# Quarters of expert products in halves, spread over the border between two blocks

## What is computed

```python
x = x + gnn(layernorm(x), edge_attr, edge_index, ...)      # stages ahead of the mixture
y = layernorm(x)                                           # then, by groups g of t = 16 rows:
logits = einsum('bgtd,des->bgtes', grouped, controller) + tie
perm   = (logits == max(logits, axis=t))                   # one row of the group per expert and set
inner  = relu(einsum of f1 (d,e,s,f=32) with the chosen rows)
inter2 = einsum('bgesf,esfd->bgesd', inner, f2)
result = einsum('bgesd,bgtes->bgtd', inter2, perm)         # back to the rows
out    = x + result
```

## Time and profile before

| | |
|---|---|
| median of 3 runs | 1958.4 us |
| the profiled execution | 1965.0 us, its span 1963.3 us |
| mean granted TensorE clock in it | 0.97 |
| TensorE busy in the span | 1824.5 us, 93% |
| VectorE, ScalarE, GpSimd busy | 1170.8, 988.4 and 356.6 us |
| mixture | from about 1150 us to the end |

### The profile page before, as it was taken

How to read it: one execution, slowest core, us unless ns; L and a number is a source line. 1 busy time by engine, 2 the same in 40 slices (tenths; PEclk the granted TensorE clock), 3 DMA queues, 4 the chain that set the end, 5 groups by cost and what they waited for, 6 DMA issues and landing times. The chain is left out here.

```text
span 1963.3 us, 40727 instructions
## 1 busy us (share of the span) xinstructions
PE 1824.5 (93%) x15580; PEld 1320.5 (67%) x15580; DVE 1170.8 (60%) x2339; ACT 988.4 (50%) x1716; POOL 356.6 (18%) x387
## 2 busy tenths in 40 slices
PE   5487699999999989999999977999999999999999
PEld 3344578888888878888888866555555565665554
DVE  6488466666666544333333336767767777777665
ACT  2355123333333366556655524766657667666653
POOL 4476220000000000000000024222223223222210
PEclk9787899999999999999999989999999999999999
DMA  9987755566666374334433357555546555556433
GB/s 368 301 163 107 169 168 167 167 177 183 180 179 179 122 275 149 126 127 162 150 125 125 116 163 242 161 156 176 163 150 196 154 164 180 164 171 181 136 111 114
DMA packets 246960, 332.09 MB, mean 169 GB/s; under 512 B 58049, under 2 KB 170177, under 8 KB 243618
## 3 DMA queue, kind: packets, MB, share of 16 engines
q1 hardware_dynamic: 237855, 309.11, 50.4%
q0 software_dynamic: 8960, 20.98, 5.6%
HBM read 189.43 MB, written 140.61 MB: 168 GB/s over the span
## 5 line engine op out<-in xcount | busy, mean ns | idle before, releaser
L1535 PE MATMUL bank<-f2s,inner_bd 128*32 128x512 f32 x2528 | 295.8, 598 | 0.6 <-issue 0.4
L599 ACT ACTIVATE h1o<-bank,b_by_channel 128x500 f32<-128x500 f32 x160 | 108.5, 678 | 324.6 <-PE bank L431 316.1
L1434 ACT ACTIVATE inter_hi<-bank 128x512 fp32r<-128x512 f32 x316 | 189.2, 599 | 162.6 <-PE bank L1535 161.6
L1356 DVE TENSOR_TENSOR inter_lo<-bank,inter_hi 128x512 fp32r<-128x512 f32 x316 | 216.2, 689 | 68.0 <-ACT inter_hi L1434 63.2
L429 PE MATMUL bank<-hhi,w_hi 128*128 128x500 f32 x624 | 244.5, 392 | 0.0
L431 PE MATMUL bank<-hhi,w_lo 128*128 128x500 f32 x624 | 243.5, 390 | 0.0
L430 PE MATMUL bank<-hlo,w_hi 128*128 128x500 f32 x624 | 242.6, 389 | 0.0
L429 PE MATMUL bank<-ahi,w_hi 128*128 128x500 f32 x608 | 237.3, 390 | 0.0
L430 PE MATMUL bank<-alo,w_hi 128*128 128x500 f32 x608 | 236.6, 389 | 0.0
L431 PE MATMUL bank<-ahi,w_lo 128*128 128x500 f32 x608 | 236.4, 389 | 0.0
L563 DVE BATCH_NORM_STATS2 stats<-h1o 128x500 f32 (+1 forms) x160 | 103.2, 674 | 155.5 <-ACT h1o L599 155.5
(11 more groups left out here) (140 smaller groups left out, 3240.7 us busy)
## 6 DMA issues: line engine op xcount, KB each, us to landing
h1T<-h1o SPq DMA_DIRECT2D x19, 2000.0 KB, 8.1
h1in<-h1T SPq DMA_DIRECT2D x19, 2000.0 KB, 9.7
aggregate<-at SPq DMA_DIRECT2D x20, 1024.0 KB, 8.9
x<-in_x SPq DMA_DIRECT2D x79, 256.0 KB, 3.2
x<-x SPq DMA_DIRECT2D x79, 256.0 KB, 3.6
back_f<-selection SPq DMA_DIRECT2D x79, 256.0 KB, 3.2
x_back<-x SPq DMA_DIRECT2D x79, 256.0 KB, 3.3
out<-x_back SPq DMA_DIRECT2D x79, 256.0 KB, 2.2
```

What stands on the lines that cost most here:

```text
L599: nc.scalar.activation(h1o[b][:, m, :], mb[m % 4][:, 0:CW], ACT.Identity, bias=b1c[:, m:m + 1]).then_inc(evr, 1)
L1356: nc.vector.tensor_tensor(ilo[b][:, :], bI[b][:, :], ihi[b][:, :].bitcast(F32), ALU.subtract).then_inc(ilr, 1)
L1434: nc.scalar.activation(ihi[b][:, :], bI[b][:, :], ACT.Copy).then_inc(ihr, 1)
L1535: last = nc.tensor.matmul(bI[b][32 * i:32 * i + 32, :], ibd[:, e, j, :, :].rearrange("p s g -> p (s g)"), f2s[:, e, :], start=True, stop=True)
```

## The change

Each quarter is done in two halves of two experts (a step "inner_head", then "inner" for the second half), only the second of which tells VectorE and ScalarE that the quarter is done. Waits stand ahead of the first half. At the borders the halves have other steps between them. For TensorE the order at a regular border becomes: sums; unit 1; unit 2; half 1a; unit 3; 1b; unit 4; 2a; turn_x; 2b; turn_g; logits; 3a; final; 3b; then spread; unit 1; 4a; unit 2; 4b; turn_g; unit 3; unit 4; and on as before. At the first border: 2a; turn_g; 2b; unit 1; 3a; unit 2; 3b; 4a; 4b; unit 3. The ReLU of quarter 2 moves ahead of the new tile's addition and statistics on VectorE, and on SyncE and VectorE turn_g and stats move behind that quarter. Quarter 4 goes to bank `bD[1]`; it waits for quarter 2's ReLU, which is long done, and for the addition of the old block's last tile. Work and its amount are the same.

```diff
--- before.py
+++ after.py
@@ -904,7 +904,7 @@
 
             return bY[::-1] if crossing(kb, j) else bY
 
-        bQ = [bD[0], bD[1], bD[0], bD[0]]
+        bQ = [bD[0], bD[1], bD[0], bD[1]]
         bL, bP = bB[:, 0:P], bB[:, 0:P]
 
         wctl, wf2 = sem("controller_loaded"), sem("f2_loaded")
@@ -1023,25 +1023,31 @@
                 if crossing(back, m):
                     if ahead:
                         yield "sums", m
-                    for p in range(3):
-                        yield "unit", u + p
-                        yield "low", u + p
-                        if p == 1 and next_:
-                            yield "norm", m + 2
+                    yield "unit", u
+                    yield "low", u
+                    yield "unit", u + 1
+                    yield "low", u + 1
+                    if next_:
+                        yield "norm", m + 2
+                    yield "inner_head", (front, 0)
+                    yield "unit", u + 2
+                    yield "low", u + 2
                     yield "inner", (front, 0)
                     yield "unit", u + 3
                     yield "low", u + 3
+                    yield "inner_head", (front, 1)
                     if next_:
                         yield "turn_x", m + 2
+                    yield "inner", (front, 1)
                     if new:
                         yield "turn_g", m + 3
                         yield "stats", m + 3
-                    yield "inner", (front, 1)
                 elif behind and m == 0 and back > 0:
                     yield "unit", u
                     yield "low", u
                     if next_:
                         yield "norm", m + 2
+                    yield "inner_head", (back, 3)
                     yield "unit", u + 1
                     yield "low", u + 1
                     yield "inner", (back, 3)
@@ -1058,18 +1064,21 @@
                     if next_:
                         yield "turn_x", m + 2
                 elif behind and m == 0:
+                    yield "inner_head", (back, 1)
+                    if new:
+                        yield "turn_g", m + 3
                     yield "inner", (back, 1)
                     yield "unit", u
                     yield "low", u
                     if next_:
                         yield "norm", m + 2
-                    if new:
-                        yield "turn_g", m + 3
-                    yield "inner", (back, 2)
+                    yield "inner_head", (back, 2)
                     yield "unit", u + 1
                     yield "low", u + 1
+                    yield "inner", (back, 2)
                     if new:
                         yield "stats", m + 3
+                    yield "inner_head", (back, 3)
                     yield "inner", (back, 3)
                     yield "unit", u + 2
                     yield "low", u + 2
@@ -1125,12 +1134,15 @@
                     yield "select", (m + 1) // 2
                 if exists(front, m + 4 + m % 2):
                     yield "silu", ((m + 4 + m % 2) // 2, (1 - m % 2) * KH // 2, (2 - m % 2) * KH // 2)
+                if crossing(back, m):
+                    yield "inner_head", (front, 2)
                 if behind:
                     yield "final", m
                     yield "result", m
                 if crossing(back, m):
                     yield "inner", (front, 2)
             if front is not None and back is None:
+                yield "inner_head", (front, 0)
                 yield "inner", (front, 0)
 
         def relu(op, q, s, *more):
@@ -1552,19 +1564,20 @@
                         nc.tensor.matmul(bF[:, :], rbd[j % 2][:, b, :], ilo[b][:, :], start=False, stop=(b == QB - 1))\
                             .then_inc(fp, 1)
 
-                def inner(k, q):
-
-                    if q == 0:
+                def inner(k, q, half):
+
+                    if q == 0 and half == 0:
                         if static(k, 1):
                             pe.wait_ge(wf1, 16 * KH)
                         pe.wait_ge(yr, (k * TB + tiles(k)) * KH)
-                    if q == 1 and not static(k, 1):
+                    if q == 1 and half == 0 and not static(k, 1):
                         pe.wait_ge(otr, k * TB - 1)
-                    if q >= 2:
-                        last = 0 if q == 2 else 2
-                        pe.wait_ge(inv, (k * QB + last + 1) * 2)
-                        pe.wait_ge(ina, (k * QB + last + 1) * 2)
-                    for e in range(QE * q, QE * q + QE):
+                    if q == 3 and half == 0 and not static(k, 1):
+                        pe.wait_ge(otr, k * TB)
+                    if q >= 2 and half == 0:
+                        pe.wait_ge(inv, (k * QB + q - 1) * 2)
+                        pe.wait_ge(ina, (k * QB + q - 1) * 2)
+                    for e in range(QE * q + half * QE // 2, QE * q + (half + 1) * QE // 2):
                         for c in range(KH):
                             for s in range(NS):
                                 es = e * NS + s
@@ -1572,7 +1585,8 @@
                                     bQ[q][32 * s:32 * s + 32, (e % QE) * 64:(e % QE) * 64 + 64],
                                     f1s[:, c, es * FF:(es + 1) * FF], yT[:, c, es, :],
                                     start=(c == 0), stop=(c == KH - 1))
-                    last.then_inc(inp, 1)
+                    if half == 1:
+                        last.then_inc(inp, 1)
 
                 def warm(n):
 
@@ -1597,8 +1611,10 @@
                             inter(k, kb, n)
                         if what == "final":
                             final(k, kb, n)
+                        if what == "inner_head":
+                            inner(*n, 0)
                         if what == "inner":
-                            inner(*n)
+                            inner(*n, 1)
 
                 blocks(pe, body)
```

## The result

The changed kernel takes 1949.8 us (median of 5 runs, 1949.35 to 1950.96) where the kernel before took 1959.1 us in as many beside it: ratio 0.995, interval 0.9938 to 0.9961, 9.4 us faster. The forecast was 1949.5. Its profiled execution took 1949.4 us, 15.6 less than that of before.

The account below looks back on a forecast made before the run. TensorE was taken as the bound, losing time to instruction supply every 256 instructions. Terms -6.9 - 2.7 + 1.5 - 1.0 - 1.6 = -10.7 us, five sixths for the median: -8.9, 1949.5 us; range 1943.5 to 1958.5.

Parts of the forecast that it names:

- Halves two and three around the last products (-6.9): Regular borders: with half the third quarter ahead, the instruction fetch precedes the data burst; pauses and half clock go, 6.9 us.
- The four named pauses: Fourth-quarter pauses behind 72, 96, 64 and 88 products at regular borders, 1.19 + 1.93 + 0.41 + 1.75 us, expected to go.
- The pause at 120 products (1.9 us and about 1 us stay): At two borders (120 products, and the one behind) the boundary stays in the burst: 1.9 and about 1 us stay.
- Spreading (-2.7): Units, transposes and logits between halves shorten small pauses at the borders from 6.7 to about 4 us; bounds 0 and 5.
- near 186: Sign that the forecast is right: the eight regular borders together take near 186 us, against 193.50 us profiled.
- The ReLU of the fourth quarter (+1.5): New block's first tile: VectorE's ReLU ends later, fourth unit short about 0.2 us; +1.5 us, bounds 0 and 5.4.
- Rival (c): Slower: VectorE bounds the first tile, ReLU 0.6 us late at all nine borders, costing 5.4 us: 1962.8 us; chance 0.08.
- The last border (-2.6): Last products' wait for the second quarter's ReLU shrinks 1.0 us, clock likely stays up, 1.6 us; bounds 0 and 2.9.
- The first border (0): Three fetches in a row at 4.2 us against about 3.4 us of work; reordering changes neither: 0.
- five sixths of the sum: Scaling from the profiled execution, 6.6 us above the median, to the median: -10.7 us becomes -8.9.
- (a): Rate, not place: fetch needs 4.2 us everywhere, only clock and last border's wait gained, about -3 us, 1955.5; chance 0.18.
- (b): Nothing moves: pauses come from the small products themselves, the split adds waits as large as it removes: 1958.4; chance 0.12.

Follow-up runs that it names:

- e_shift: The kernel before with 12 more warm-up products (48 TensorE instructions) at the start of the mixture: 1966.5 us in one run, regular borders 189.4 us together.
- before_again: The kernel before, unchanged, run once more for a second profile: 1964.2 us in its profiled run, regular borders 187.8 us together.
- third profile of the changed kernel: The changed kernel, unchanged, run again as reference on the same chip as e_late_new: ratio 0.9957 to the kernel before, regular borders 183.3 us together.
- e_small: The kernel before with the old block's last-tile store and the two loads behind it cut to 16 of 128 partitions: ratio 0.9966.
- e_late_old: The kernel before with only the two loads of each block's first tile issued later on SyncE, behind the new tile's store: ratio 0.9977.
- e_late_new: The changed kernel with the same two loads issued later, as in e_late_old: ratio 0.9954 to the kernel before.
- e_rest: The changed kernel with the third quarter whole again behind the last products, all else as in the change: ratio 0.9990 to the kernel before.
- e_third: The kernel before with only the third quarter in two halves, the first ahead of the last products, the second behind: ratio 0.9968.
- e_padold: The kernel before with already satisfied waits added between borders, so all eight regular borders meet the instruction-block boundary where the sixth did: ratio 0.9973.

## Why the prediction was right, and where it wasn't

**What bounds the kernel: right.** The pauses are instruction supply at a distance of 256 instructions. e_shift shows it, the profile after agrees. The sign given for it, "issue" near 5 us at the expert products, came out (5.1), but partly by luck: what is left was forecast at the first, fourth and fifth border, and 3.85 us of it stand at the first, 1.4 more than before, only 0.2 at the fourth and nothing at the fifth.

**Halves two and three around the last products (-6.9): the mechanism was right and incomplete.** The boundary was to fall 0.3 to 0.8 us behind the end of the last products and its packet ahead of the burst; it fell at 0.7 and the packet was ahead. The four named pauses and the clock loss are gone in that profile. In before_again three of the four stand (1.5, 1.1 and 1.0 us, none behind 88) and there is no clock loss at a regular border, so 1.6 us of the term belong to one profile; in the third profile of the changed kernel 0.7 us behind 96 are back. What was incomplete is the sentence that "no such packet started while data took 82.8%", read as one cause. At the third border the wait on the third quarter's ReLU, which I costed at 0 in the change of bank, was a second one, of nearly the same length. Had the burst been the only cause there, e_small and e_late_old would have cleared the border; they left 1.1 and 1.4 us. At borders 2 and 7 the burst alone was enough. The change removes the wait and moves the boundary ahead of the burst. How a wait holds back a packet isn't seen in the records: packets start about 1 us behind the ReLU in two kernels. At the second border of before the boundary is at 1371.9, the ReLU for which the last products wait ends at 1373.21, these products start at 1373.57, and the packet at 1374.61, 1.4 us behind the ReLU and 1.0 behind their start. That the request is made only when the engine has got past the wait is my reading. It was not isolated: no run has the kernel before with both causes away and its order kept. And the change takes the burst out of the way only where the packet wins its race: in the third profile of the changed kernel, and in e_late_new against the store alone (+2.0 us), it did not.

**The pause at 120 products (1.9 us and about 1 us stay): too pessimistic.** The fourth border takes 22.94 us instead of 24.55, so about 0.8 us are left of lost time. The fifth, which had 1 us behind its quarter, takes 22.11. The two other profiles agree: 23.1 and 23.1, 22.6 and 22.2.

**Spreading (-2.7):** with the two terms before, -9.6 was forecast for the sum, or -8.1 with the ReLU's +1.5: "near 186". The first pair of profiles gives -13.4 (180.1), the mean of all gives -9.3. e_rest bounds the spreading alone: 0.1%, about 2 us, interval -0.4 to 4.3, and its sum of 188.5 is no lower than before_again's. So the size isn't shown, nor that it is more than nothing.

**The ReLU of the fourth quarter (+1.5): mis-sized, it costs 0.** The fifth regular border of the changed kernel, TensorE and VectorE, which answers the earlier trace rows:

```profile
1606.16 1.09 PE L1584 MATMUL bank<-yT,f1s 128*32 128x64 f32 x64
1607.18 0.65 PE L1472 MATMUL bank<-ident,h2in 128*128 128x128 f32 x4
1607.77 1.92 PE L1547 MATMUL bank<-f2s,inner_bd 128*32 128x512 f32 x16
...
1607.05 0.69 DVE L1368 TENSOR_TENSOR inter_lo<-bank,inter_hi 128x512 fp32r<-128x512 f32 x1 [0.61 <-ACT inter_hi L1446]
1607.65 0.85 DVE L1150 TENSOR_SCALAR inner_bd<-bank 32x256 f32<-32x256 f32 x2
```

The queue is as forecast: the low part runs just behind the quarter, the ReLU behind it, and ends at 1608.50 (1607.65 + 0.85), 1.4 us behind the quarter's end. I had 1.5 and said that 0.2 would be missing. The fourth unit starts at 1607.77 + 0.86 = 1608.6, so 0.1 us is to spare, and the 16 products of the two units take the undisturbed 1.92 us. Only at the last border does the unit wait, 0.5 us. Rival (c) had its mechanism right and was 0.1 us short of its threshold.

**The last border (-2.6): right, the clock's part by luck.** 20.8 us became 18.5. The wait for the ReLU is 0.4 instead of 1.27, the clock is 1.00 behind it, and a fetch pause of 0.65 us stays. But before_again has this border at full clock too, at 20.3 us, with a fetch pause of 1.5 us instead. On the mean of the profiles 20.6 became 18.5. e_third alone brings 18.3: it is the half of the third quarter ahead of the last products.

**The first border (0): right.** Three pauses of 1.0 to 1.4 us stay; 18.75 us against 17.7 and 20.3 in the two profiles of before; the other two of the changed kernel have 18.2 and 17.9.

**Sum and scaling.** Forecast against the profiled execution -10.7, measured -15.6: 13.4 less at the regular borders, 2.3 at the last, 1.0 more at the first, 0.9 elsewhere. The median moved by 9.4. So the number was right, in part by luck, with two errors that cancel: the profiled execution of before was heavier than I allowed for with five sixths of the sum (its regular borders took 5.7 us more than in the next profile; 9.4 is 0.6 of 15.6), and the difference of the profiles was larger than the terms. Rivals: (a), rate alone, is refuted by the regular borders at 22.1 us with the same work; (b) by e_shift and by the result; (c) by the row above.

## What to carry to other kernels

Where dense small products pause with no semaphore as releaser, count instructions between the pauses; if the distance is constant it is supply, and both a data burst and a semaphore wait just behind a boundary can delay the next packet, so look for the second cause before pricing the first. Half a dense stretch moved ahead of the burst was worth more here than even spreading, and about as much as padding the kernel before (0.9968 against 0.9973). Ask how much time a fetch has left before the burst: here the packet and the burst started within 0.3 us of each other in two profiles, and where the packet came later the pause was back. Take the size of pauses from more than one profiled execution: their places repeat, their lengths don't.

## What the runs showed of the hardware

- A wait that is already satisfied costs TensorE no visible time in the tiles' passes. With 24 of them, 12 instructions, in a tile's pass (e_padold) the first units of successive tiles start at 1400.01, 1407.71 and 1416.58; without them, in the kernel before, at 1398.43, 1406.14 and 1415.01: 7.7 and 8.9 us in both.
- Start to start, a 64-column product with its load comes every 15.4 ns or faster in a quarter (128 in 1.97 us), with four groups of 32 columns in turn. The Trainium skill, page "TensorE: Matmul & The Clock Gate", section "Wait — 56ns, not 53.3ns?", says that start-to-start never drops below about 25 ns however small the product is. The trace disagrees for products that take the four groups in turn; no run here has one group alone.
- The clock after a stop isn't set by the stop's length alone. In the profile of before the stop of 1.93 us was followed by 3.4 us at 0.50, the stop of 1.91 us at the next border by 3.4 us at full clock, though the clock was full ahead of both:

```profile
1540.40:1543.80 3.40, 3.40 (x36) 1.71 (x36) 2.70 (x5) 2.20 (x5) 0.00 (x0) 1.00 0.45 126
```

  So here a stop of this size put about 1.6 us at risk and didn't always cost them. Removing it removes the risk.
